# Attention 1: exponentials and the two halves of the probabilities taken over two quarters in one operation

## The reference

```python
q = (query @ Wq).reshape(b, sq, NUM_HEADS, HEAD_DIM).transpose(0, 2, 1, 3)   # 32 heads of 16
k = (key @ Wk).reshape(b, sk, NUM_KV_HEADS, HEAD_DIM).transpose(0, 2, 1, 3)  # 8 heads, each used 4 times
...
scores = jnp.einsum('bhqd,bkhd->bhqk', q, k) * scale
probs = jax.nn.softmax(scores, axis=-1)
out = jnp.einsum('bhqk,bkhd->bqhd', probs, v)
...
return out @ Wo
```

## Time and profile before

| | |
|---|---|
| median of 3 runs | 1602.65 us (1600.28 to 1606.68) |
| the profiled execution | 1601.44 us, span 1599.7 us |
| granted TensorE clock, mean over the span | 0.975 |
| scores of attention 1, first and last tile | 1356.2 and 1499.3 us |
| exponentials L1789 | 64, 38.3 us |
| high halves L1795 | 64, 36.3 us |
| low halves L1565 | 64, 72.7 us |

### The profile page before, as it was taken

One profiled execution on the slowest core, in us unless ns is written; L12 is line 12 of the kernel. 1 busy time (PEld: TensorE's weight loads), 2 busy tenths in 40 slices (PEclk: granted clock), 3 DMA queues, 4 the chain that ended last, 5 costly groups with the idle time before them and its releaser, 6 DMA issues. The chain is left out here.

```text
span 1599.7 us, 29290 instructions
## 1 busy us (share of the span) xinstructions
PE 1481.6 (93%) x11214; PEld 779.1 (49%) x11214; DVE 1257.5 (79%) x2249; ACT 845.3 (53%) x1773; POOL 303.5 (19%) x271
## 2 busy tenths in 40 slices
PE   6999999999999999999999987799999998678678
PEld 3555555555555555555555443344444445344344
DVE  4878876677777777677777787988888885999877
ACT  3554562343433433433424432688888863888742
POOL 0032130011111102010111100011111102789730
PEclk9999999999999999999999998999999999999889
DMA  6276573214331231414132232132223350776502
GB/s 250 80 175 169 139 179 79 80 54 106 65 93 53 60 110 28 121 47 118 52 105 57 49 119 94 50 47 47 47 52 58 63 100 1 146 106 111 104 1 106
DMA packets 317163, 140.77 MB, mean 88 GB/s; under 512 B 265873, under 2 KB 290577, under 8 KB 316818
## 3 DMA queue, kind: packets, MB, share of 16 engines
q1 hardware_dynamic: 273954, 98.15, 28.5%
q10 hardware_dynamic: 43120, 41.42, 8.3%
HBM read 66.13 MB, written 11.53 MB: 49 GB/s over the span
## 5 line engine op out<-in xcount | busy, mean ns | idle before, releaser
L639 PE MATMUL xp<-WO,OT 128*128 128x512 f16 x1536 | 344.2, 385 | 7.8 <-DVE X L924 7.8
L600 PE MATMUL pj<-XT,WQ 128*128 128x512 f16 x1536 | 340.4, 381 | 5.5 <-DVE WQ L285 4.9
L639 PEld LDWEIGHTS xp<-WO,OT 128*128 128x128 f16 x1536 | 149.1, 99 | 194.1 <-issue 24.8
L600 PEld LDWEIGHTS pj<-XT,WQ 128*128 128x128 f16 x1536 | 148.6, 98 | 182.5 <-issue 9.0
L757 ACT ACTIVATE E<-E 128x512 f32<-128x512 f32 x64 | 40.2, 628 | 292.2 <-DVE E L902 292.2
L1163 PE MATMUL db<-W0T,XD 128*128 128x448 f16 x768 | 155.4, 361 | 10.6 <-ACT db L1263 7.4
L1181 PE MATMUL eb<-W1T,DT 128*128 128x512 f16 x672 | 149.0, 381 | 3.9 <-ACT eb L1273 3.9
L924 DVE SCALAR_TENSOR_TENSOR X<-xp,X 128x512 f32<-128x512 f32 x128 | 88.2, 689 | 78.4 <-PE xp L639 77.3
L574 POOL TENSOR_TENSOR VW<-VW,XB 128x1024 f32<-128x1024 f32 x14 | 33.0, 2357 | 601.9 <-DVE VW L103 601.9
L862 DVE SCALAR_TENSOR_TENSOR QT<-pj,QT 128x512 f16<-128x512 f32 x128 | 88.0, 687 | 70.4 <-ACT QT L727 70.4
L1163 PEld LDWEIGHTS db<-W0T,XD 128*128 128x128 f16 x768 | 75.1, 100 | 87.8 <-ACT db L1263 13.0
(11 more groups left out here) (240 smaller groups left out, 2433.8 us busy)
## 6 DMA issues: line engine op xcount, KB each, us to landing
W0T<-in_L_xattn_wo ACTq DMA_DIRECT2D x15, 1024.0 KB, 5.3
W0T<-in_L_xattn_wq SPq DMA_DIRECT2D x9, 1024.0 KB, 5.4
W0T<-in_L_xattn_wq ACTq DMA_DIRECT2D x7, 1024.0 KB, 6.2
X<-in_x SPq DMA_DIRECT2D x4, 1024.0 KB, 7.5
XB<-in_L_ffn_W ACTq DMA_DIRECT2D x28, 128.0 KB, 3.0
w0t<-XB ACTq DMA_DIRECT2D x7, 512.0 KB, 7.5
w1t<-W0T ACTq DMA_DIRECT2D x7, 512.0 KB, 7.7
W0T<-w0t ACTq DMA_DIRECT2D x1, 3584.0 KB, 11.7
```

What stands on the lines that cost most here:

```text
L600: last = pe.matmul(bank[:, :], w, src[:, b, k, tokens], start=n == 0, stop=n == 3 * KC - 1)
L639: last = pe.matmul(xp[i % 2][:, :], OT[:, a, j, i * P:(i + 1) * P], WO[:, b, j, :], start=n == 0, stop=n == 3 * REP - 1)
```

## The change

The exponentials, the high halves and the low halves are each taken over a half of the tile (two quarters, 1024 columns) in one operation, where they were taken over a quarter (512 columns). The waits count accordingly. The exponential of a half waits for both subtractions of the half. The high half, which stood behind one other instruction after its own exponential, follows it directly. Subtractions, sums and DMA transposes keep their sizes.

```diff
-                        sp.wait_ge(S[split], 4 * t + 2 * h + 2)
+                        sp.wait_ge(S[split], 2 * t + h + 1)
...
-            def low_probs(t, q):
-                pool.wait_ge(S["e_hi"], 4 * t + q + 1)
+            def low_probs(t, h):
+                own = slice(2 * h, 2 * h + 2)
+                pool.wait_ge(S["e_hi"], 2 * t + h + 1)
                 if t >= 1:
-                    pool.wait_ge(S[f"pt{q // 2}_done"], 32 * t)
-                pool.tensor_tensor(EH[:, 1, q, :], E[:, q, :, :].rearrange("p u n -> p (u n)"), EH[:, 0, q, :],
+                    pool.wait_ge(S[f"pt{h}_done"], 32 * t)
+                pool.tensor_tensor(EH[:, 1, own, :], E[:, own, :, :].rearrange("p q u n -> p q (u n)"), EH[:, 0, own, :],
                                    ALU.subtract).then_inc(S["e_lo"], 1)
...
-            def exp(t, q):
-                act.wait_ge(S["sub_done"], 4 * t + q + 1)
-                act.activation(E[:, q, :, :], E[:, q, :, :], ACT.Exp, scale=exp_scale).then_inc(S["exp_done"], 1)
+            def exp(t, h):
+                own = slice(2 * h, 2 * h + 2)
+                act.wait_ge(S["sub_done"], 4 * t + 2 * h + 2)
+                act.activation(E[:, own, :, :], E[:, own, :, :], ACT.Exp, scale=exp_scale).then_inc(S["exp_done"], 1)
...
-            def high_probs(t, q):
-                act.wait_ge(S["exp_done"], 4 * t + q + 1)
+            def high_probs(t, h):
+                own = slice(2 * h, 2 * h + 2)
+                act.wait_ge(S["exp_done"], 2 * t + h + 1)
                 if t >= 1:
-                    act.wait_ge(S[f"pt{q // 2}_done"], 32 * t)
-                act.activation(EH[:, 0, q, :], E[:, q, :, :].rearrange("p u n -> p (u n)"), ACT.Copy).then_inc(S["e_hi"], 1)
+                    act.wait_ge(S[f"pt{h}_done"], 32 * t)
+                act.activation(EH[:, 0, own, :], E[:, own, :, :].rearrange("p q u n -> p q (u n)"), ACT.Copy).then_inc(S["e_hi"], 1)
...
                     exp(t, 0)
-                    exp(t, 1)
                     high_probs(t, 0)
-                    high_probs(t, 1)
                 if 1 <= t <= TILES:
                     spread_out(t - 1)
                 if t < TILES:
-                    exp(t, 2)
-                    exp(t, 3)
-                    high_probs(t, 2)
-                    high_probs(t, 3)
+                    exp(t, 1)
+                    high_probs(t, 1)
...
             def less_max(t, q, scores):
                 dve.wait_ge(S["max_done"], 4 * t + q + 1)
                 if t >= 1:
-                    dve.wait_ge(S["e_lo"], 4 * (t - 1) + q + 1)
+                    dve.wait_ge(S["e_lo"], 2 * (t - 1) + q // 2 + 1)
...
-                dve.wait_ge(S["exp_done"], 4 * t + 2 * h + 2)
+                dve.wait_ge(S["exp_done"], 2 * t + h + 1)
```

More of the change, by code:

```diff
@@ L1630, in _ @@
                 if t < TILES:
-                    for q in range(4):
-                        low_probs(t, q)
+                    for h in range(2):
+                        low_probs(t, h)
                 if t + 2 < TILES:
```

## The result

The changed kernel took 1609.84 us (median of 9 runs, 1607.41 to 1617.79), the kernel before 1602.26 (9 runs, 1599.74 to 1606.68). The ratio is 1.0053, 95% interval 1.0042 to 1.0064: 8.5 us more, 6.7 to 10.3. The change makes the kernel slower by about half a per cent. The forecast was 1609.9 us and 0.46%.

What follows compares the result with a forecast made beforehand. It took a ring through PE, DVE and ACT to bind tiles 2 to 7, and DVE with ACT the other ten. 2.8 + 4.4 + 0.1 = 7.3 us gave 1608.7, plus 1.2 for the median 1609.9; range 1605.5 to 1613.6.

Steps and rivals of the forecast that it cites:

- ACT's chain, tiles 2 to 7, 0.47 each: Merged exponential and high half start `spread_out` 0.47 us later, lengthening the ring through PE: 6 x 0.47 = 2.8 us.
- Rival 2: Tiles 2 to 7: POOL's `normal` releases `transposes`, so they pay only 0.18 us each; 1608.2 us in all; chance 0.12.
- DVE with ACT's second half, ten tiles, 0.44 each: Tiles 0, 1, 8 to 15: `high`, and DVE's `low` waiting for it, come 0.44 us later: 4.4 us.
- The 0.1 us for tile 13: Added because POOL's `low_out`, which releases `project_out` there, comes 1.0 us later instead of DVE's 0.88.
- At 7.83 of 10 us the clock was 1.00, and the new tiles lower that share only by a twentieth: Argument from PE's busy share in a steady tile against its clock falling in one more tile.
- rival 3: PE's clock falls in one more tile, bringing the sum to at least 8.0 us: 1610.8 to 1613.6 us; chance 0.20.
- a sign of being wrong: The changed kernel's profile showing PE's clock at half speed in tiles that had full speed.
- the second case of rival 3: One fall of PE's clock in tiles 2 to 7, costing up to 3.7 us, so 1613.6 us.
- Rival 1: If ACT bound the stage, 64 merges would save 0.08 us each: 5.1 us, 1597.5 us; chance 0.05.
- Rival 4: The hop between two dependent ACT operations is 0.10 us: 1.8 us more, 1611.7 us; chance 0.13.

Runs made afterwards that it cites:

- spread_first: The changed kernel with `spread_out` of the previous tile moved ahead of the first exponential on ACT: 1600.34 us, ratio 0.9988 to the kernel before.
- before_spread: The kernel before with `spread_out` of the previous tile moved between the first and second exponential on ACT: 1597.60 us, ratio 0.9971.
- exp_only: The kernel before with only the exponentials merged over halves, high and low halves still over quarters: 1611.38 us, ratio 1.0059.
- high_only: The kernel before with only the high halves merged, exponentials and low halves still over quarters: 1605.58 us, ratio 1.0011.
- low_only: The kernel before with only POOL's low halves merged: 1603.05 us, ratio 1.0004.
- changed_beside: The changed kernel measured once more with no further edit: 1611.23 us, ratio 1.0060 to the kernel before.

## Why the prediction was right, and where it was not

**ACT's chain, tiles 2 to 7, 0.47 each.** Right: 0.48 in tiles 3 to 7, made of the terms as given (1.06, 1.06, a hop of 0.03, one lost overlap). The length that the Trainium skill gives for it (ScalarE: Activation LUTs, What ACT_TABLE_LOAD costs), 1.04 us, is 0.01 to 0.02 short of the measured 1.05 and 1.06. The prediction says that by this length its sum would be 0.5 us smaller; worked through its own steps it is about 1.0 (0.04 in six tiles and 0.08 in ten), an estimate. That `spread_out` is the gate, against the name in the profile, was shown by `spread_first` for the changed kernel and by `before_spread` for the one before. Rival 2 falls.

**DVE with ACT's second half, ten tiles, 0.44 each.** Right for tiles 0, 1 and 8 to 11, within 0.01. For tiles 12 to 14 the sum is 1.68 against 1.4, spread unevenly by the clock. For tile 15 only the whole tail is known, 0.79 against 0.44.

**Which part costs.** The prediction put all of it on ACT's chain; `exp_only` (1.0059), `high_only` (1.0011) and `low_only` (1.0004) bear that out. What the change gives up is the cover of the first exponential, which ran while DVE still subtracted: the merged one starts where the second one did (3.12 and 3.11 us after the first maximum). No run merged the exponentials of the second half alone, which would have kept this cover; that the cover and not the second half carries the cost rests on these starts.

**POOL.** Mis-sized, without effect: 2.13 us instead of 2.36. The 0.1 us for tile 13 can't be found again, since the slow projection moved to tiles 12 and 14; no run shows that term.

**"At 7.83 of 10 us the clock was 1.00, and the new tiles lower that share only by a twentieth"** is the step that failed; with it the sum left out rival 3. It took tile 5 for all of tiles 2 to 7, and 1.4 us for PE's idle time ahead of `transposes`. In tile 2 this idle time was already 1.60 us and grew to 2.09. The clock fell there in both profiles of the changed kernel and in that of `exp_only` (2.18 us), which the prediction named as a sign of being wrong. It did not fall there in `high_only` (1.66 us), with an early `spread_out`, or in the two profiles where fillers left 1.23 us. So the fall follows from the change, and the fillers show that the idle time ahead of `transposes` is what makes it. But the length of one idle time doesn't decide alone: in tile 10 of the changed kernel PE is idle for 2.11 us ahead of `spread`, and `project` runs at full speed behind it (2.75 us), while behind the same 2.11 us it takes 4.44 in both profiles with the fillers. What decides there stays open. In tile 2 the fall costs 1.7 us beyond the 0.48. That is the second case of rival 3, at less than half of the 3.7 that it gave as the most. In tiles 12 to 15 one or two slow projections were there before the change and are after it; they move between tiles (13 before; 12 and 14 in one profile of the changed kernel, mainly 13 in the other) and tiles 12 to 14 together grew by 1.68 us in the one and by 1.06 in the other, around the forecast.

**Why the number was still met.** Between the two profiles the fifteen tiles grew by 8.9 us and the tail by 0.8, together 2.4 more than the 7.3 forecast. Two things hid this. The stages ahead were 1.3 us shorter in the profiled run, by scatter: the first maximum of tile 0 lay between 1354.3 and 1362.1 us over the profiles of this case, in stages that no edit touched. And the forecast added 1.2 us for the median over the profiled execution, while in the changed kernel the two are the same. So the agreement of 1609.9 with 1609.84 is luck; what the prediction had right is the cost of eleven tiles. The better estimate of the whole cost is the ratio, 8.5 us (6.7 to 10.3), and it can't tell 7.3 from the 9.0 that it would be with tile 2. Of the tail's 0.79 us, 0.45 is there before the last layer's norms, as forecast. The other 0.34 is in one operation on DVE (L155, 128x4), which took 1.12 us instead of 0.78 beside an addition on POOL (L1577, before L1576), and in both profiles ended 0.02 or 0.03 us after it. It took 0.17 us in `changed_beside`, whose tail was no shorter (99.35), so this part moves between executions; its cause was not tried.

Rival 1 (ACT's saving shows) is refuted: ACT was busy for 3 us less and nothing came of it. Rival 4 (a hop of 0.10) as well: the hop is 0.03. The lower end of the range, 1605.5, is a slip: rival 2 less the scatter shown is 1608.2 - 2.4 = 1605.8.

## What to carry to other kernels

Merging small operations shortens the work of one engine, and that shows only if this engine binds. Where a producer or a consumer works in step with the small operations, the merge takes away cover; here that was 0.44 to 0.48 us a tile, against 3 us in all that ACT was busy for less. Cost such an edit from the last input that it waits for to the first result that somebody needs. When a wait has several semaphores, check each candidate's end against the start, not the name. And the same reading that prices an edit shows where the order is wrong: two moves into existing waits gave 0.57%, about as much as the change lost (0.53%).

## What was not expected of the hardware

- PE's clock fell to 1.2 GHz in tile 2 when its idle time ahead of `transposes` grew from 1.60 to 2.09 us, and not in tiles 3 to 7, where it grew from 0.93 or 0.95 to 1.41; four unused matmuls of 512 columns in the gap kept it at 2.4 GHz. In both profiles with them it fell in tile 10, which cost 0.24 us.
- A float32 less float16 subtraction of 1024 columns took POOL 2.13 us, against 2 x 1.16 for two of 512 and 2.36 for the float32 one in the earlier trace rows.
- The start of attention 1 varied by 8 us between profiles, in code that didn't change, while tiles 0 to 11 of the changed kernel repeated to 0.02 us between its two profiles. Tiles 12 to 14 did not: each moved by 0.2 to 1.1 us with the clock. For edits of half a per cent in a late stage, the lengths of the steady tiles tell more than the times of a few executions.
